# Attention in groups of two heads on row halves, with the maxima on one pair of PSUM banks

## The reference

```python
q = (x @ Wq + bq).reshape(B, S, H, HD)          # H = 16, HD = 8, S = 512
k, v = ctx @ Wk + bk, ctx @ Wv + bv             # 154 rows, and 64 more in L0
attn = jax.nn.softmax(einsum('bhsd,bhtd->bhst', q, k) * scale, axis=-1)
out = einsum('bhst,bhtd->bhsd', attn, v).reshape(B, S, D) @ Wo + bo
```

## Time and profile before

| | |
|---|---|
| median of 3 runs | 1137.58 us (1133.59 to 1139.87) |
| profiled execution | 1143.49 us, its span 1141.7 us |
| granted TensorE clock, mean | 0.918 of full speed |
| busy share of the span | PE 89%, PEld 61%, DVE 50%, ACT 38%, POOL 24% |
| matmuls and weight loads | 5652 each |
| DVE and ACT instructions | 1368 and 777 |

### The profile page before, as it was taken

How to read it: one execution, slowest core, us unless ns; L and a number is a source line. 1 busy time by engine, 2 the same in 40 slices (tenths; PEclk the granted TensorE clock), 3 DMA queues, 4 the chain that set the end, 5 groups by cost and what they waited for, 6 DMA issues and landing times. The chain is left out here.

```text
span 1141.7 us, 15533 instructions
## 1 busy us (share of the span) xinstructions
PE 1021.3 (89%) x5652; PEld 695.5 (61%) x5652; DVE 571.6 (50%) x1368; ACT 432.2 (38%) x777; POOL 269.9 (24%) x394
## 2 busy tenths in 40 slices
PE   2899999988789999989999989999989999999985
PEld 2644454336555544468887764544478888888774
DVE  3644645433345465454553445555464545444458
ACT  3164544343316445533242235553532323222240
POOL 8220112234415343310021013331210101000044
PEclk9889999787669899899999899889799999999997
DMA  5000000000010110000000011100000000000001
GB/s 137 3 1 13 1 13 2 12 1 16 1 68 1 32 31 2 30 20 1 1 1 1 1 40 43 44 25 15 26 6 1 1 1 1 1 1 1 1 1 38
DMA packets 27149, 18.11 MB, mean 16 GB/s; under 512 B 5793, under 2 KB 25345, under 8 KB 26946
## 3 DMA queue, kind: packets, MB, share of 16 engines
q1 hardware_dynamic: 27074, 17.12, 5.4%
HBM read 15.64 MB, written 1.05 MB: 15 GB/s over the span
## 5 line engine op out<-in xcount | busy, mean ns | idle before, releaser
L1100 DVE TENSOR_REDUCE mneg<-PS 128x2 f32<-128x308 f32 (+1 forms) x384 | 184.0, 517 | 167.7 <-PE PS L725 161.5
L1512 ACT ACTIVATE work<-PS 124x512 f32<-124x512 f32 (+1 forms) x272 | 160.1, 605 | 151.0 <-PE PS L806 150.3
L1246 DVE TENSOR_TENSOR work<-PS,work 128x512 f32<-128x512 f32 (+2 forms) x168 | 114.8, 685 | 175.4 <-PE PS L863 129.8
L1537 ACT ACTIVATE work<-PS 128x512 f32<-128x512 f32 (+2 forms) x168 | 99.9, 596 | 258.2 <-PE PS L863 245.9
L880 PEld LDWEIGHTS PS<-down_w,work 128*128 128x128 f32 (+2 forms) x1472 | 176.3, 195 | 6.3 <-DVE work L1246 1.3
L880 PE MATMUL PS<-down_w,work 128*128 128x128 f32 (+2 forms) x1472 | 176.2, 277 | 1.0 <-DVE work L1246 1.0
L861 PE MATMUL PS<-xh_sb,arena 128*128 128x512 f32 (+2 forms) x352 | 149.4, 424 | 10.4 <-DVE work L1246 9.6
L1607 POOL TENSOR_SCALAR rstd<-bn_mv 128x4 f32<-128x4 f32 x32 | 8.7, 271 | 585.3 <-DVE bn_mv L1024 585.1
L863 PE MATMUL PS<-xh_sb,arena 128*128 128x512 f32 (+2 forms) x352 | 142.5, 405 | 0.0
L862 PE MATMUL PS<-xl_sb,arena 128*128 128x512 f32 (+2 forms) x352 | 141.8, 403 | 0.0
L725 PE MATMUL PS<-kb_sb,qxt_sb 97*128 97x308 f32 x256 | 88.5, 393 | 19.8 <-DVE mneg L1100 15.6
(11 more groups left out here) (168 smaller groups left out, 1301.6 us busy)
## 6 DMA issues: line engine op xcount, KB each, us to landing
ctx_rep<-in_ctxT SPq DMA_DIRECT2D x12, 308.0 KB, 3.3
stage<-in_w SPq DMA_DIRECT2D x8, 256.0 KB, 4.1
stage<-in_wg SPq DMA_DIRECT2D x8, 176.0 KB, 2.3
stage<-in_wu SPq DMA_DIRECT2D x8, 176.0 KB, 2.4
x_res<-in_x SPq DMA_DIRECT2D x4, 256.0 KB, 3.9
down_w<-in_w SPq DMA_DIRECT2D x1, 1024.0 KB
down_w<-in_wd SPq DMA_DIRECT2D x8, 128.0 KB
out<-x_res SPq DMA_DIRECT2D x4, 256.0 KB, 2.3
```

Source lines behind the costliest of these rows:

```text
L1100: dve.tensor_reduce(mneg[:, a % 2, t, h0:h0 + 2], PS[:, mx_bank(i_main, m), 0:2 * (KT0 if layer == 0 else KC)].rearrange("p (h n) -> p h n ...
L1246: dve.tensor_tensor(HH[0:rows, e % 2, j, :], PS[0:rows, 2 * (n % 2) + 1, :], SS[0:rows, n % 2, :], ALU.mult).then_inc(*sig["h"].mark((i, n)))
L1512: act.activation(P[0:rows, n % P_RING, :], PS[0:rows, n % 2, :], ACT.Exp, scale=SCALE).then_inc(*sig["p"].mark((i, n)))
L1537: act.activation(SS[0:rows, n % 2, :], PS[0:rows, bank, :], ACT.Silu).then_inc(*sig["act"].mark((i, n)))
```

## The change

Heads go in 8 groups of 2, two groups (f = 0, 1) at a time: one on partitions 0 to 50 of `QXT` and the key array, the other on 64 to 114. So K has 49 rows for a maximum (51 for a score), and a pair of matmuls on the two row halves fills two banks. Keys are padded to 156 and interleaved by head. A block has 110 rows (55 keys x 2 heads) in layer 0 and 104 in layers 1 and 2, 4 and 3 blocks per group: 16 and 12 pairs an item, in 32 and 24 slots, one pair every second slot, in banks 0, 1 and 2, 3 in turn. One exponential covers a pair, 1,024 columns. The value blocks get two columns of ones beside the 16 of a group's values, so the same product gives the sums; the product with the mask falls away, and the quads alternate between banks 6 and 7.

There are 16 maxima per item, a pair of matmuls and one reduction of two banks each. In items the pair is always 4 and 5, which the transposes of queries, keys and x, the projections, the value blocks and the transposed maxima use too. Their slots are 5 + m * (N - 4) // 16.

At the end of an item ACT copies banks 6 and 7 to `RAW` (slot N + 3). SP moves the 16 rows of sums to `DEN` (8 DMAs, 128 partitions x 64) and the value rows to `VP` (8 DMAs). In the next item DVE takes the reciprocal of `DEN` (slot 2 of an attention item), SP spreads it over `RB` (8 DMAs), DVE multiplies (slot 6) and `finish` comes at slot 8. In F0 these are slots 0, 1 and 2, in F1 and F2 slots 1, 3 and 4.

The bias of v moves into the bias of the output (`value_bias`: one matmul and one addition per layer), so v's blocks are one matmul each and one more in the memory rows of layer 0; the replicated context `CR` with its 12 loads goes, and a context that holds each column twice is loaded at the start (`ctxR`). Key copies on ACT (`kb_out`) are 2 instead of 4 per item, the mask rows written by `shift_rows` come from the transposes, and more arrays are set at the start (`KX`, `VB`). The DMAs of the maxima are 8 per item instead of 4.

```diff
-PR = HL * 3 * HD
+KP = 156
+HB = 2
+PR = HB * 3 * HD
+HALF = 64
+X_ROWS = HALF + K_ALL
-N_MAX = 2 * G * T
+N_MAX = G * T
-P_RING = 8
-R0, C0 = 125, 7
-R1, C1 = 124, 5
-KT0 = KC + KM
+P_RING = 4
+R0, C0 = 55, 4
+R1, C1 = 52, 3
+KT0 = KP + KM
...
 def n_slots(i):
-        return 4 * chunk_shape(layer)[1]
+        return 2 * G * chunk_shape(layer)[1]
...
-            put(6, "finish", i - 1)
+            put(2, "recip", i - 1)
+            put(6, "normal", i - 1)
+            put(8, "finish", i - 1)
...
         if is_attn(i - 1):
-            put(2, "finish", i - 1)
+            put(0 if short else 1, "recip", i - 1)
+            put(1 if short else 3, "normal", i - 1)
+            put(2 if short else 4, "finish", i - 1)
...
         def qxt_bank(i_main, g):
-            return (2 if i_main is not None and ITEMS[i_main][0] == "A" else 4) + g % 2
+            return 4 + g % 2
...
         def mt_bank(i_main, part):
-            return 2 if part and i_main is not None and ITEMS[i_main][0] == "A" else 4
+            return 4
...
         def mx_bank(i_main, m):
             if i_main is None:
-                return (0, 1, 2, 3, 6, 7)[m % 6]
-            return (2 if ITEMS[i_main][0] == "A" else 4) + m % 2
+                return (0, 2, 6)[m % 3]
+            return 4
...
+            def denominators_out(sp, i):
+                sp.wait_ge(*sig["raw"].at(i))
+                if i > 0:
+                    sp.wait_ge(*sig["rden_in"].at(last_attention(i)))
+                for j in range(2 * G):
+                    bank, row = j // 4, 32 * (j % 4)
+                    sp.dma_start(DEN[16 * j:16 * j + 16, :],
+                                 RAW[row + 16:row + 18, bank, :].rearrange("p (s n) -> p s n", s=8)).then_inc(*sig["den_in"].more(i))
+                if i > 0:
+                    sp.wait_ge(*sig["o_psum"].at(last_attention(i)))
+                for j in range(2 * G):
+                    bank, row = j // 4, 32 * (j % 4)
+                    sp.dma_start(VP[16 * j:16 * j + 16, :], RAW[row:row + 16, bank, :]).then_inc(*sig["v_in"].more(i))
+
+            def reciprocals_out(sp, i):
+                sp.wait_ge(*sig["rden"].at(i))
+                if i > 0:
+                    sp.wait_ge(*sig["on"].at(last_attention(i)))
+                for d in range(HD):
+                    sp.dma_start(RB[d:128:HD, :].rearrange("p (s n) -> p s n", s=8), DEN[:, :]).then_inc(*sig["rden_in"].more(i))
...
             def scores_for_max(i_main, a, m):
-                w = 2 * (KT0 if layer == 0 else KC)
-                pe.matmul(PS[:, bank, 0:w], QXT[0:KX_ROWS, a % 2, g, t * 128:(t + 1) * 128],
-                          KB(layer)[0:KX_ROWS, a % 2, g, f * w:(f + 1) * w], start=True, stop=True).then_inc(*sig["mx_psum"].mark((a, m)))
-                taken[bank] = sig["mx"].at((a, m))
+                for f in range(2):
+                    if bank + f in taken:
+                        pe.wait_ge(*taken[bank + f])
+                    taken[bank + f] = sig["mx"].at((a, m))
+                w = HB * head_width(layer)
+                for f in range(2):
+                    half = slice(HALF * f, HALF * f + KX_ROWS)
+                    mm = pe.matmul(PS[:, bank + f, 0:w], QXT[half, a % 2, g, t * 128:(t + 1) * 128], KB(layer)[half, a % 2, g, 0:w],
+                                   start=True, stop=True)
+                mm.then_inc(*sig["mx_psum"].mark((a, m)))
...
             def attention_step(i, n):
+                if n % 2 == 0 and n < N:
+                    m = n // 2
+                    c, g = m // G, m % G
+                    bank = 2 * (m % 2)
+                    for f in range(2):
+                        mm = pe.matmul(PS[0:HB * rows, bank + f, :], chunk_columns(layer, a % 2, g, f, c),
+                                       QXT[HALF * f:HALF * f + K_ALL, a % 2, g, :], start=True, stop=True)
+                    mm.then_inc(*sig["st"].mark((i, m)))
                 if n % 4 == 1 and n >= 5:
+                    u = (n - 5) // 4
+                    c, bank = u // 2, 6 + u % 2
+                    for r in range(4):
+                        j = 4 * (u % 2) + r
+                        mm = pe.matmul(PS[32 * r:32 * r + 32, bank, :], VB[0:HB * rows, a % 2, c, j, :], P[0:HB * rows, j // 2, j % 2, :],
+                                       start=(c == 0), stop=(c == chunks - 1))
+                    mm.then_inc(*sig["pv"].mark((i, u)))
-                if n % 4 == 3 and n >= 7:
-                    for g in range(G):
-                        pe.matmul(PS[32 * g:32 * g + 32, 7, :], mask[0:rows, c, :], P[0:rows, (4 * c + g) % P_RING, :],
-                                  start=(c == 0), stop=(c == chunks - 1)).then_inc(*sig["dn"].mark((i, 4 * c + g)))
...
             def maxima(i_main, a, m):
-                dve.tensor_reduce(mneg[:, a % 2, t, h0:h0 + 2],
-                                  PS[:, mx_bank(i_main, m), 0:2 * (KT0 if layer == 0 else KC)].rearrange("p (h n) -> p h n", h=2),
+                dve.tensor_reduce(mneg[:, a % 2, t, g * HL:(g + 1) * HL].rearrange("p (f h) -> p f h", f=2),
+                                  PS[:, bank:bank + 2, 0:HB * head_width(layer)].rearrange("p f (n h) -> p f h n", h=HB),
                                   AX.X, ALU.max, negate=True).then_inc(*sig["mx"].mark((a, m)))
...
-            def attention_end(i):
-                dve.wait_ge(*sig["dn"].at((i, n_slots(i) - 1)))
-                dve.reciprocal(ON, PS[:, 7, :]).then_inc(*sig["rden"].mark(i))
-                dve.wait_ge(*sig["rden"].at(i))
-                dve.tensor_tensor(ON, PS[:, 6, :], ON, ALU.mult).then_inc(*sig["on"].mark(i))
+            def reciprocals(i):
+                dve.wait_ge(*sig["den_in"].at(i))
+                dve.reciprocal(DEN[:, :], DEN[:, :]).then_inc(*sig["rden"].mark(i))
+
+            def normalise(i):
+                dve.wait_ge(*sig["v_in"].at(i))
+                dve.wait_ge(*sig["rden_in"].at(i))
+                dve.tensor_tensor(VP[:, :], VP[:, :], RB[:, :], ALU.mult).then_inc(*sig["on"].mark(i))
...
+            def exps(i, m):
+                act.activation(P[0:rows, m % P_RING, :, :], PS[0:rows, 2 * (m % 2):2 * (m % 2) + 2, :], ACT.Exp, scale=SCALE).then_inc(*sig["p"].mark((i, m)))
+
+            def evacuate(i):
+                act.wait_ge(*sig["pv"].at((i, last_quad(i))))
+                act.activation(RAW[:, :, :], PS[:, 6:8, :], ACT.Copy).then_inc(*sig["raw"].mark(i))
```

More of the change, by code:

```diff
@@ L99, in weight_chunks, with last_pair, last_quad, last_attention @@
     return [(m, e * F2, F2) for e in range(E2) for m in range(2)] + [(m, E2 * F2, FS) for m in range(2)]
+def last_pair(i):
+    return n_slots(i) // 2 - 1
+def last_quad(i):
+    return n_slots(i) // 4 - 1
+def last_attention(i):
+    return max(n for n in range(i) if ITEMS[n][0] == "A")
 def last_expert(kind):
@@ L130, in plan @@
     nxt = i + 1
+    if i + 2 < len(ITEMS) and ITEMS[i + 2][0] == "A" and ITEMS[i + 2][2] == 0:
+        put(0, "bv", ITEMS[i + 2][1])
     if i + 2 < len(ITEMS):
@@ L139, in plan @@
                 put(0, "kt", a1)
-            for h in range(HL):
+            for h in range(HB):
                 put(h, "kb", a1, h)
@@ L655, in v_blocks @@
-            def v_blocks(a, part):
+                taken[4] = taken[5] = sig["kb"].at((a, HB - 1))
+            def v_blocks(a):
                 layer, b = a // B, a % B
                 rows, chunks = chunk_shape(layer)
-                if part == 0:
-                    pe.wait_ge(*sig[f"cr_in{a % 2}"].at(a))
-                    if a == 0:
-                        pe.wait_ge(*sig["mem_ready"].at(0))
-                        pe.wait_ge(*sig["const_in"].at(0))
-                pe.wait_ge(*taken[4 + part])
-                for c in range(4 * part, min(4 * part + 4, chunks)):
-                    o = PS[0:rows, 4 + part, (c % 4) * D:(c % 4 + 1) * D]
-                    cols = slice(c * rows, (c + 1) * rows)
-                    mem = layer == 0 and (c + 1) * rows > KC
-                    pe.matmul(o, CR[:, a % 2, cols], WA[:, layer % 2, 2, :], start=True, stop=False)
-                    ind = IND0[:, cols] if layer == 0 else IND0[:, 0:rows]
-                    mm = pe.matmul(o, ind, BVr[:, layer, :], start=False, stop=not mem)
+                if a == 0:
+                    pe.wait_ge(*sig["mem_ready"].at(0))
+                    pe.wait_ge(*sig["const_in"].at(0))
+                pe.wait_ge(*taken[4])
+                for c in range(chunks):
+                    o = PS[0:HB * rows, 4, c * D:(c + 1) * D]
+                    cols = slice(c * HB * rows, (c + 1) * HB * rows)
+                    mem = layer == 0 and (c + 1) * rows > KP
+                    mm = pe.matmul(o, ctxR[:, b, cols], WA[:, layer % 2, 2, :], start=True, stop=not mem)
@@ L674, in v_blocks, with value_bias @@
                     if mem:
                         mm = pe.matmul(o, MR[:, cols], ident[:, :], start=False, stop=True)
-                mm.then_inc(*sig["v_psum"].mark((a, part)))
```

(21 more changed lines are left out.)

407 lines of the change are left out of this document (190 added, 217 removed).

## The result

The changed kernel takes 1330.95 us, median of 4 runs (1328.95 to 1334.98), the kernel before beside it 1137.21 (1133.59 to 1139.87): ratio 1.171, 95% interval 1.167 to 1.175. I forecast slower, 1186, in a range of 1105 to 1235. It is 145 us slower than forecast. Some executions are over 1.5% longer than the fastest of their kernel; medians here are of all, ratios leave those out, which matters most for e15 (0.982 by the medians, 0.978 by the ratio).

A forecast was written before the change was run, and what follows sets the result against it. TensorE was taken to bound the kernel; its saving would be eaten by the maxima's bank loop and a DMA loop. Terms -4 - 4.3 + 34 + 1 + 10 - 3 + 13 + 10 - 8 = +48.7, about 1186 us, range 1105 to 1235.

The forecast's parts named there:

- start: Kernel's start: fewer, wider maxima and fewer copies against larger loads and memsets; -8 us, together with the last F0, F1 maxima.
- A: Rival, faster: SP issues cheap enough (0.34 us) to hide the loop through DMAs; -28 us, 1110; chance 0.18.
- D: Rival, a draw: a DMA issue costs 0.48 us, shortening the loop in 12 places; 1144; chance 0.07.
- B: Rival: the maxima's strided PSUM reduction costs twice the slope; +104 us at most, about 1280; chance 0.07.
- Term 1: Maxima on one bank pair: serial loop of 1.30 us (layer 0 1.62) eats most of PE's saving; b = 0 -4, -4.3.
- rival C: Halves of a pair run in turn (+43 us), or TensorE more often at 1.2 GHz; about 1225; chance 0.13.
- Term 1, ends: Parts around an item's maxima: 7.2 us of ACT's queue ahead, 4.4 behind (5.3 in layer 0).
- Term 2, b = 1 and 2: Product waiting on 24 DMAs stalls DVE 6.7 us (6.1 in layer 0); +34 for four items, +1 layer 0.
- Term 2, b = 3 and transitions: PE waits for the DMA loop at the out-projection: b = 3 +10 and -3, F0 +13, F1 and F2 +10.

The follow-up runs named there:

- e15: Changed kernel with maxima in own banks released singly, loop DMAs on two queues, some added TensorE work, later FFN product and projection: 1125.3 us, 0.978 of before.
- e4: Changed kernel plus small zero products on TensorE behind each maximum and where it waits for the DMA loop: 1260.8 us, 1.107 of before.
- e10: Changed kernel with maxima of b = 0, 1, 2 in banks 2 and 3, their score pairs all in 0 and 1: 1271.5 us, 1.118 of before.
- e5: Changed kernel without the 24 DMAs between exponential sums and output projection, so division and gathering are missing: 1241.7 us, 1.088 of before.
- e2: Changed kernel with product in slot 12 and output projection in slot 14 of attention items: 1319.2 us, 1.157 of before.
- e8: Changed kernel with half of the loop's DMAs moved from SP to GpSimd's queue: 1279.9 us, 1.121 of before.
- e16: Changed kernel with only the product and output projection in later slots of F0, F1 and F2: 1308.3 us, 1.146 of before.

## Why the prediction was wrong

By stages, forecast and measured against before: nine items with maxima +26.7 and +137.7; b = 3 with the FFN stages +30 and +55.6; start -8 and -5.2. So 111 of the 139 us missing lie in the nine items. By parts of an item, forecast and measured, the nine summed: from the first exponential to the first load for the maxima 64.8 and 87.1; from there to the last reduction's end 312.2 and 380.1; behind it 42.3 and 63.1. The sign, slower, came out right in part for a reason that I didn't have: I had the three b = 0 items at 8.3 us less than before, and they took 39.7 more.

1. **Single costs** were right: exponential 1.02 (1019 ns), reductions 0.80 and 1.07 (806 and 1071), DMAs of the loop (eight issued in 5.07 us, 0.63 each), the product's place. So rivals A and D are out, which wanted issues of 0.34 and 0.48 us, and B too: the reduction of every second float costs what a contiguous one does (806 against the 799 of the earlier trace rows).
2. **Term 1, the step that failed.** The terms of the loop (0.45, 0.80, 0.05) are from the earlier trace rows, where PE was at 2.4 GHz, and the sentence behind them has scores and quads fit in, "as 1.07 plus 0.2 is under 1.30". Even at that level the loop was 0.10 too short (1.40 and 1.72, by 0.03 in the first part, 0.01 in the reduction and 0.06 in the last), and a quad did not fit in quite (1.78 in e4, with added work in it). At 1.2 GHz neither holds: the turns were 1.62 and 1.99, not 1.30 and 1.62, and 2.43 and 2.93 around a quad. First load to last reduction's end: 37.4 in b = 0 of layer 1 and 44.5 of layer 0 against 28.6 and 32.8. Most of that is the lower clock's work, as e4 shows: the two items fall from 56.1 and 63.5 to 46.4 and 52.0, and over the nine items the middle part gives back 48 of its 68 us and the part behind the maxima 20 of its 21. So what the prediction put at nothing in its sum is TensorE's level. I had the mechanism as half of rival C, with a chance of 0.13 and a price of 40 us; that price was never worked out from an item. A reader can do it: the quad of 1.07 in the earlier trace rows is some 2 us at half the clock and then longer than the turn, so PE sets the pace in six or eight turns of sixteen, and the gaps keep the level down.
3. **Term 1, ends.** Ahead of the maxima I added up ACT's queue alone, 7.2; it was 9.1 to 10.9 to the first load. The transposes of the queries idle PE for 28 us in all behind ACT's key copies, which go through the same banks, and ACT's copies then wait for them. No run undoes this: the part ahead stays at 86 to 87 us with the sharing of the maxima undone (e10), with added work (e4) and without the loop (e5), so that this is its cause is argued and not shown. Behind the maxima it was 5.9 to 8.1 against 4.4 and 5.3, chiefly by the clock (3.9 to 5.5 in e4).
4. **Term 2, b = 1 and 2.** Mechanism right, size too large: DVE's stall was 3.1 to 5.3 in the six items (3.4 and 5.3 in layer 1), not 6.1 and 6.7, as the second maximum came later. Leaving the loop out gains 3.4 and 4.8 in the two of layer 1. The queue behind it that counts as much is SP's: the stage DMAs (e2, e8).
5. **Term 2, b = 3 and transitions.** +55.6 against +30. I let the exponentials run on at 1.04 after the projection. In b = 3 of layer 2 they don't:

```profile
1001.82 1.94 ACT L1561 ACTIVATE work<-PS 104x1024 f32<-104x1024 f32 x2 [1.56 <-PE PS L852]
1002.90 0.20 PEld L867 LDWEIGHTS PS<-work,vb_sb 104*32 104x32 f32 x8 [1.46 <-ACT work L1561]
1002.90 1.94 PE L867 MATMUL PS<-work,vb_sb 104*32 104x512 f32 x8 [0.69 <-ACT work L1561]
...
1006.64 1.94 PE L867 MATMUL PS<-work,vb_sb 104*32 104x512 f32 x8 [1.12 <-ACT work L1561]
```

Two quads are 3.74 us apart instead of 2.08: quad, scores and two exponentials take turns, as PE stands at the quad until its exponential is done and issues no scores meanwhile. Over these three stretches two queues give back 33 us (e8), the later slots 21 (e16) and leaving the loop out 62 (e5), the added work only 1 (e4): here it is the loop that I priced too low, not the clock of the nine items.

6. **Halves and quads.** The halves of a pair do start together: at 2.4 GHz a pair takes 0.41 (471.90 above), where in the kernel before one matmul of 308 columns takes 0.41 and two in turn 0.56:

```profile
408.81 0.41 PE L725 MATMUL PS<-kb_sb,qxt_sb 97*128 97x308 f32 x1
...
410.37 0.56 PE L725 MATMUL PS<-kb_sb,qxt_sb 97*128 97x308 f32 x2
```

So rival C's other half, halves in turn, is out. The Trainium skill's page TensorEngine Tiling (Array Packing), Key Properties, has a change of tiling mode drain the engine. The trace agrees at the quads: the next load starts at 441.12, as a quad ends (441.19 by its modelled end), 1.66 us after the loads of the quad. It was so before too (the next scores at 480.67, the quad's end at 480.75), so this is no new cost of a switch; it grows with the quad, from 1.07 to 1.93.

What stays open: how the 138 us of the nine items divide between sharing, joint release, clock and DMA loop. Singly undone they give 62, 40, 70 and 24 of them, 196 in all, so they overlap. That each one's gaps lower the clock for the others would explain it; that was not taken apart.

## What to carry to other kernels

Price a chain between two engines with the durations of TensorE's lower level as well, and ask which level the gaps of that very chain will leave it at: here a turn that was 1.40 became 1.62, and 2.43 with a quad. A pair of PSUM banks that is filled, read and released as one is a single buffer; release its halves singly. A saving on the busiest engine that is bought with waits of that engine can cost more than it saves, and the same layout came out ahead (0.978 against 1.171) once its maxima had banks of their own, released one by one, its DMAs two queues, its product a later slot and PE a little useless work in the gaps.
